# Chain sums of edge tiles by matrix products in a graph attention kernel's last loop bodies

## What is computed

```
q, k, v = layer_norm(x_node @ Wq), ... per head;  ke, ve = layer_norm(x_edge @ Wke), ...
rel_k = layer_norm(concat(ke, k[src]) @ relk_W + relk_b);  rel_v the same from ve, v
qk  = sum(q[dst] * rel_k, -1) / 4
m   = segment_max(qk, dst);  se = segment_sum(exp(qk - m[dst]), dst);  lse = log(se) + m
h   = (qk - lse[dst]) * rel_v
agg = segment_sum(h, dst)
z   = layer_norm(relu(agg @ z_W + z_b));   out = _layernorm(x + z)
```

## Time and profile before

| | us |
|---|---|
| median of 3 runs | 2994.78 (2994.47 to 2997.76) |
| profiled execution | 2993.24 |
| its span | 2991.5 |
| first instruction of `edges` (POOL) | 188.55 |
| first instruction of the tail (POOL's memset) | 2758.62 |
| first gather of sums | 2794.80 |
| first gather of log-sums | 2883.24 |

### The profile page before, as it was taken

The page is one execution under the profiler, slowest core; times in us unless marked ns, Lnnn a source line. Parts: engine busy times, 40 slices in busy tenths (PEclk is TensorE's granted clock), DMA queues, the critical chain, the costliest instruction groups (busy, mean ns, idle before and its releaser), DMA issues. The chain is left out here.

```text
span 2991.5 us, 74825 instructions
## 1 busy us (share of the span) xinstructions
PE 2805.4 (94%) x18870; PEld 2486.7 (83%) x18870; DVE 2848.9 (95%) x3072; ACT 2304.7 (77%) x5301; POOL 2396.4 (80%) x2622
## 2 busy tenths in 40 slices
PE   4669999999999999999999999999999999998945
PEld 3349999999999999999999999999999999996633
DVE  6879999999999999999999999999999999998948
ACT  2448888888888888888888888888888888886527
POOL 6768888888888888888888888888888888885773
PEclk8989999999999999999999999999999999999978
DMA  4568888888888888888888888888888888887742
GB/s 89 163 177 242 258 255 257 253 256 252 255 253 257 254 254 253 255 254 255 253 255 253 255 254 254 256 253 251 257 255 253 256 252 254 254 264 215 196 112 56
DMA packets 661200, 703.01 MB, mean 235 GB/s; under 512 B 98801, under 2 KB 555238, under 8 KB 660749
## 3 DMA queue, kind: packets, MB, share of 16 engines
q1 hardware_dynamic: 568897, 491.48, 54.4%
q0 software_dynamic: 84896, 208.11, 25.5%
q10 hardware_dynamic: 7340, 2.66, 0.5%
HBM read 470.00 MB, written 231.15 MB: 234 GB/s over the span
## 5 line engine op out<-in xcount | busy, mean ns | idle before, releaser
L1446 POOL DMA_INDIRECT e_rows<-node_table,e_gcol x1564 | 1911.9, 1222 | 420.2 <-issue 416.1
L1239 PE MATMUL banks<-w_edge,e_eat 128*128 128x240 f32 x6256 | 1397.0, 366 | 0.5 <-ACT e_ysq L1368 0.5
L1239 PEld LDWEIGHTS banks<-w_edge,e_eat 128*128 128x128 f32 x6256 | 1180.6, 190 | 84.5 <-issue 0.7
L1218 PE MATMUL banks<-e_h,e_oh 128*128 128x248 f32 x3128 | 782.9, 373 | 2.9 <-DVE e_h L1552 2.8
L1547 DVE TENSOR_REDUCE e_zs<-e_z 128x96 f32<-128x1440 f32 x391 | 642.7, 1644 | 0.2
L1218 PEld LDWEIGHTS banks<-e_h,e_oh 128*128 128x128 f32 x3128 | 563.5, 190 | 44.9 <-DVE e_h L1552 4.3
L1331 ACT ACTIVATE e_agg<-banks 128x496 f32<-128x496 f32 x782 | 458.0, 586 | 109.9 <-PE banks L1218 103.9
L1535 DVE TENSOR_TENSOR e_p<-banks,e_yr 128x960 f32<-128x960 f32 x391 | 452.5, 1157 | 27.6 <-PE banks L1239 13.7
L1552 DVE TENSOR_TENSOR e_h<-e_p,e_zw 128x960 f32<-128x960 f32 x391 | 449.5, 1150 | 1.2 <-POOL e_zw L1459 1.2
L1346 ACT ACTIVATE e_eat<-banks 128x512 f32<-128x512 f32 x391 | 233.4, 597 | 281.5 <-PE banks L1252 281.5
L1516 DVE TENSOR_TENSOR e_p<-e_p,e_rows 128x960 f32<-128x960 f32 x391 | 449.6, 1150 | 0.0
(11 more groups left out here) (414 smaller groups left out, 2607.2 us busy)
## 6 DMA issues: line engine op xcount, KB each, us to landing
tile_sums<-e_agg SPq DMA_DIRECT2D x391, 496.0 KB
e_q<-q_by_rank SPq DMA_DIRECT2D x1564, 90.0 KB
e_ea<-in_edge_attr SPq DMA_DIRECT2D x390, 256.0 KB
e_rows<-node_table,e_gcol POOLq DMA_INDIRECT x1564
edge_lse<-t_lse_sb SPq DMA_DIRECT2D x14, 448.0 KB, 3.5
edge_qk<-e_qkt SPq DMA_DIRECT2D x130, 48.0 KB
node_table<-n_tb SPq DMA_DIRECT2D x24, 240.0 KB, 2.6
n_x<-in_x SPq DMA_DIRECT2D x24, 128.0 KB, 2.3
```

Source lines behind the costliest of these rows:

```text
L1218: last = nc.tensor.matmul(sums_bank(x, loop, half)[:, (j % 2) * AW:(j % 2 + 1) * AW], oh[:, x % OR, j, :], hh[:, x % HR, j, :, :].rearrang ...
L1239: last = nc.tensor.matmul(out_ps[:, j // 2, (j % 2) * 2 * HC:(j % 2 + 1) * 2 * HC], eat[:, x % 4, j * P:(j + 1) * P], t["w_edge"][:, at:at ...
L1446: g.indirect_dma_start(out=rows[:, k, j, :], out_offset=None, in_=table, in_offset=bass.IndirectOffsetOnAxis(ap=gcol[:, kb, at:at + 1].bit ...
```

## The change

The scans over transposed rows give way to matrix products. Two matrices of 128x128 zeros and ones say for a set which of its tiles are in the same chain up to a tile, and which are in the chain that the last tile of the set before belongs to; they come by comparing a row of chain numbers (`seg_row`, the same in all partitions) with a column of them (`seg_col`, `last_col`). POOL makes them with 25 comparisons (`make_mats`), PE multiplies (`chain_sum`, one product for set 0 and two for the others), ACT copies the sums back over `firsts`, and POOL adds them to `tile_sums` (`add_set`). Sets 0 to 11 do this in bodies 391 to 400 and directly behind them, set 12 in the tail. The chain numbers are stored and loaded as a column in `start`; their broadcast to all partitions stands in body 385, and first rows are loaded two sets a body from there.

In the tail, the fourth load of scores waits for nothing, the fifth also for the last set's products (the matrices lie where it lands), the sixth for seven running maxima instead of the adds. The log-sum rows of the last three steps go to three pairs of banks: step 11 to banks 0 and 1, step 12 to 2 and 3, step 13 to 4 and 5. The last running sum stands ahead of the carries, the last two logarithms ahead of the last three copies.

```
 def chain_mats(t, k):
+    at = PARTS[3][1] * SUB + 2 * P * k
+    return t["x"][:, at:at + P], t["x"][:, at + P:at + 2 * P]
+def chain_sum(nc, t, k, bank):
+    same, last_same = chain_mats(t, k)
+    out = bank[:, (k % 2) * 2 * P:(k % 2) * 2 * P + AW]
+    done = nc.tensor.matmul(out, same, t["firsts"][:, k, :], start=True, stop=(k == 0))
+    if k:
+        done = nc.tensor.matmul(out, last_same, t["firsts"][:, k - 1, :], start=False, stop=True)
+def chain_copy(sc_, t, k, bank):
+    return sc_.activation(t["firsts"][:, k, :], bank[:, (k % 2) * 2 * P:(k % 2) * 2 * P + AW], mybir.ActivationFunctionType.Copy)
...
-CHAIN_AT = GROUPS + 3
+CHAIN_AT = GROUPS + 1
...
+                kk = 2 * (c - FIRSTS_AT)
+                if not loop and kk == 0:
+                    sp.dma_start(seg_row[:].rearrange("p k e -> p (k e)"), t["chain_d"].partition_broadcast(P)).then_inc(s_more, 16)
...
+            def chain_set(k):
+                pe.wait_ge(s_cl, k + 1)
...
+                if k:
+                    pe.wait_ge(s_cbc, k)
+                chain_sum(nc, t, k, agg_ps).then_inc(s_cs, 1)
...
-                if not loop and 0 <= c - CHAIN_AT < 4:
+                if not loop and c >= CHAIN_AT:
                     chain_set(c - CHAIN_AT)
...
+            def make_mats(k):
+                same, last_same = chain_mats(t, k)
...
+                ins = g.tensor_scalar(out=same, in0=seg_row[:, k, :], scalar1=seg_col[:, k:k + 1], scalar2=None, op0=ALU.is_equal)
+                if k:
+                    ins = g.tensor_scalar(out=last_same, in0=seg_row[:, k, :], scalar1=last_col[:, k - 1:k], scalar2=None, op0=ALU.is_equal)
+                ins.then_inc(s_cl, 1)
+            def add_set(k):
+                pool.wait_ge(s_cbc, k + 1)
+                pool.reg_add(last_sum, sums_less_2, 1)
+                chain_add(nc, t, k, last_sum).then_inc(s_add, 16)
...
+                k = c - GROUPS
+                if not loop and k >= 0:
+                    for k_ in range(2 * k, min(2 * k + 2, KT)):
+                        make_mats(k_)
+                    if k >= 2:
+                        add_set(k - 2)
             every(pool, body, GROUPS + 9)
+            for k in range(GROUPS + 9 - GROUPS - 2, KT - 1):
+                add_set(k)
...
-                if k == 3:
-                    sp.wait_ge(s_cb, 7)
                 if k == 4:
                     sp.wait_ge(s_m, 4)
+                    sp.wait_ge(s_cs, KT)
                 if k == 5:
-                    sp.wait_ge(s_add, 16 * KT)
+                    sp.wait_ge(s_m, 7)
...
+    def rows_bank(k):
+        return {NSUB - 3: 2 * ((NSUB - 2) % 2), NSUB - 2: 2 * ((NSUB - 1) % 2)}.get(k, 4)
...
             v.tensor_copy(out=ends[:, 0:1], in_=m[:, CE:CE + 1]).then_inc(s_end, 1)
+            run_sum(NSUB - 1)
+            dve.wait_ge(s_s, NSUB)
+            v.tensor_copy(out=ends[:, 2:3], in_=x[:, CE - 1:CE]).then_inc(s_end, 1)
...
-            run_sum(NSUB - 1)
-            dve.wait_ge(s_s, NSUB)
-            v.tensor_copy(out=ends[:, 2:3], in_=x[:, CE - 1:CE]).then_inc(s_end, 1)
...
+            ln_of(NSUB - 2)
+            ln_of(NSUB - 1)
+            copy_lse(NSUB - 3)
             act.wait_ge(s_ab, 2)
             sc_.activation(ab, ab, ACT.Exp).then_inc(s_abx, 1)
-            ln_of(NSUB - 2)
-            copy_lse(NSUB - 3)
-            ln_of(NSUB - 1)
             copy_lse(NSUB - 2)
```

More of the change, by code:

```diff
@@ L148, in chain_back @@
[L148 to L166, removed]
@@ L637, in _ @@
             v.tensor_copy(out=rank_o[:], in_=key_f[:, 0, :]).then_inc(s_ro, 1)
+            v.scalar_tensor_tensor(out=tq[:, 0, :], in0=key_f[:, 0, :], scalar=2.0, in1=linked, op0=ALU.mult, op1=ALU.add).then_inc(s_tq, 1)
             link(v.tensor_scalar(out=base[:], in0=loc[:, 1, :], scalar1=car_ps[:, 1:2], scalar2=None, op0=ALU.max))
@@ L1413, in body @@
                     nc.scalar.activation(zw[:, x % WR, :, :, 0], zln[:, :, 1:2 * H:2], ACT.Exp, scale=-0.5).then_inc(s_zw, 1)
-                if not loop and 0 <= c - CHAIN_AT < 4:
+                if not loop and c >= CHAIN_AT:
                     copy_set(c - CHAIN_AT)
             every(act, body, GROUPS + 10)
-            for kk in range(4, len(CHAIN_SETS)):
-                copy_set(kk)
-            for kk in range(4):
-                act.wait_ge(s_cb, kk + 1)
-                chain_copy(nc.scalar, t, (2 * kk, 2 * kk + 1), banks[:, 6 + kk % 2, :]).then_inc(s_cbc, 1)
+            for k in range(GROUPS + 10 - CHAIN_AT, KT - 1):
+                copy_set(k)
         @block.gpsimd
@@ L1501, in _ @@
             link(v.tensor_copy(out=p_f, in_=p_i[:, 1:3]))
+            link(v.scalar_tensor_tensor(out=last_col[:], in0=seg_col[:], scalar=1.0, in1=ident[:, P - 1:P].to_broadcast([P, KT]), op0=ALU.add, op1=ALU.mult))
+            link(v.tensor_scalar(out=last_col[:], in0=last_col[:], scalar1=-1.0, scalar2=None, op0=ALU.add))
             link(v.tensor_copy(out=same_c[:], in_=c_i))
@@ L1563, in _ @@
             every(dve, body, GROUPS + 9)
-            dve.wait_ge(s_more, 16)
-            dve.wait_ge(s_cc, 4)
-            for half in range(2):
-                chain_scan(v, t, 0, half).then_inc(s_cs, 1)
-            dve.wait_ge(s_cs, 2)
-            dve.wait_ge(s_cc, len(CHAIN_SETS))
-            for half in range(2):
-                chain_scan(v, t, 1, half).then_inc(s_cs, 1)
     ph.close([])
@@ L1690, in _ @@
             pool.reg_add(last_sum, sums_less_2, 1)
-            for k in range(KT):
-                pool.wait_ge(s_cbc, k // 2 + 1)
-                g.indirect_dma_start(out=t["sums_d"], out_offset=bass.IndirectOffsetOnAxis(ap=t["carry_idx"][:, k:k + 1].bitcast(u32), axis=0),
-                                     in_=back[:, k, :], in_offset=None,
-                                     bounds_check=last_sum, oob_is_err=True, compute_op=ALU.add).then_inc(s_add, 16)
+            pool.wait_ge(s_cbc, KT)
+            chain_add(nc, t, KT - 1, last_sum).then_inc(s_add, 16)
             pool.wait_ge(s_add, 16 * KT)
@@ L1799, in _ @@
                 v.tensor_tensor(out=ratio[:, k % RS, :], in0=ratio[:, k % RS, :], in1=fresh[:, lo:hi], op=ALU.add).then_inc(s_d, 1)
-                if k == 0:
-                    dve.wait_ge(s_cc, 7)
-                    dve.wait_ge(s_cs, 4)
-                    for half in range(2):
-                        chain_scan(v, t, 2, half).then_inc(s_cs, 1)
                 if k >= 1:
@@ L1981, in _ @@
             sc_ = nc.scalar
[L1982 to L1984 removed]
             load_fresh(3)
+            act.wait_ge(s_cs, KT)
+            chain_copy(sc_, t, KT - 1, bank[6]).then_inc(s_cbc, 1)
             act.wait_ge(s_bias, 1)
```

152 lines of the change are left out of this document (65 added, 87 removed).

## The result

The changed kernel takes 3008.94 us (median of 5 runs, 3007.68 to 3010.48), the kernel before 2994.78: 14.2 us more, a ratio of 1.0046 (95% interval 1.0035 to 1.0056). Forecast were 2987 and a range up to 2997. The time lies outside the range, and the sign is wrong too.

What follows compares the result with a forecast made beforehand. DVE and PE bound the loop; in the tail POOL decided when log-sum gathers begin. Gain 11.2 - 3 - 0.5 = 7.7 us gave 2985.5, with the runs' median 1.5 higher 2987; likeliest 2983 to 2990, 80% 2978 to 2997.

Steps and rivals of the forecast that it cites:

- Part 3: End of the edge loop: 28.6 us of new POOL work against 25.8 free, so the tail starts 3 us later.
- Part 2: Log-sums in the tail: their last store decides, first log-sum gather 113.3 us after the tail's start instead of 124.5.
- T0: Start of the tail, DVE's first memset there; 2758.7 us before, forecast 3 us later.
- (a): POOL's new work overruns the loop's end: tail starts 14 to 18 us later, time 2998 to 3002; chance 0.12.
- (d): POOL's comparisons and DVE's instructions exclude each other at the loop's end: 7 us more, time 2994; chance 0.20.
- the gap: DVE near the tail's eighth step, ended by PE: a loss of 5.3 us from the third score load's new wait.
- the end's gain: End of the tail: three pairs of banks let the last log-sum copy end 3.5 us earlier.
- the room of 0.3: Slack in us between the third log-sum copy's end and PE's start on the next rows, subtracted from the delay.
- the start of the tail: Chain scans leave DVE, two products join PE: taken as zero, bounds 2 us of gain and 1 of loss.
- Part 1: POOL's tail: twelve of 13 adds leave, gathers of sums run from 12 to 108 us after the tail's start.
- G: First log-sum gather in the tail, forecast 113.3 us after the tail's start, with 108.3 from there to the end.
- Part 4: The rest: a store, a load and three tiny DVE instructions early on cost 0.5 us.

Runs made afterwards that it cites:

- experiment 3: The changed kernel without the sixth load's wait for the seventh running maximum; 3001.87 us, ratio 1.0023 to the kernel before.
- mended versions: Five variants of the changed kernel without the sixth load's new wait, last set's product behind the first step, comparisons and adds placed differently; 2988.16 to 2992.72 us.
- experiment 4: The changed kernel with the last set's product and its copy behind the tail's first log-sum step, run twice; 2998.59 and 3000.46 us.

## Why the forecast was wrong

**Part 3 is the step that failed most**, by 9.8 of some 22 us, and Part 2 second, by 8.0. With Part 3 right and the rest as measured the time would still have been about 2999, past the range. Part 3 failed by price and by window. The price: "I take 0.40" for a comparison, with 0.67 as the upper bound. Alone it takes 0.60; in the queue 0.89, as in five of the seven bodies one or two stand behind `e_h` or the row addition. 25 cost 22.3 us and not 10. The adds were priced well (1.3 in a body, forecast 1.55). The window: I set 28.6 us of work against 25.8 free in the stretch up to T0, but 15.9 of these lie behind POOL's last small product, where comparisons, which PE needs before, and half of the adds can't use them. Before that product there was this (window; its length, POOL's busy us and count; clock, DMA):

```profile
2712.70:2742.70 30.00, 17.90 (x24) 1.00 0.57 181
```

12.1 us were free. Ahead of it came 22.3 us of comparisons and six adds of 1.3 to 2.0, 8.5: 30.8 in all, 18.7 more than was free. DVE's last `e_h` was 18.2 us later. (The match is closer than the count deserves: 9.5 of the 12.1 are waits for ACT, the rest are gaps at issues, which a comparison can't fill, while small products that had been stretched to 1.1 to 2.0 us no longer were.)

With my own two prices in the right window the sum would have been 10 + 9.3 - 12.1, so 7.2 us late instead of the 2.8 that I had: the window is 4.4 us of the miss. The price of the comparison is 12.3, of which 5.0 are the 0.60 and 7.3 the meetings with DVE; the adds give back 0.8.

T0 moved by 12.6 only (without the 3.4 from before the loop), since 10.3 us and not 15.9 lie between that `e_h` and T0. I had allowed at most 1 us for this. SP's last issue came 7.6 us behind the last `e_h` instead of 14.2; ACT's wait of 3.87 us for a store and DVE's last two chain scans, in front of which it had waited 4.01 us for ACT, are gone. Which of the two gives how much isn't shown.

**Rivals (a) and (d)** were one mechanism. Rival (d) had the lock-step right and its size too: 7 us, measured 7.3. The way to it was another: it counted a chance of 0.46 a comparison and 0.6 us each, while the meeting occurs in every body here in which POOL has no wait left and its comparisons stand right behind the product that releases `e_h`, and costs nearly the whole of `e_h`, 1.2 us of it. That agrees with the rule of the Trainium skill, "SBUF — State Buffer", section "Who interferes with whom", that a DVE instruction with two SBUF inputs and a GpSimd instruction that reads SBUF exclude each other. The rival's T0, 10 us late, and its 2994 fell short because the 0.40, the window and the tail stayed as forecast in its sum. Rival (a) had the size of T0 and the right verdict on it (14 to 18, measured 15.9 with 3.4 from before the loop), but I gave it 0.12 and put its condition at the wrong place: what counts is the room up to POOL's last small product, not the sum up to T0. That its T0 came true is partly luck, since its adds of 2.25 us took 1.3; and its time, 2998 to 3002, stayed 7 us short, as it had none of the tail's losses.

**Part 2.** Right: the log-sums' last store decides, the gap's place, the wait of 8 us, the end's gain (3.9; forecast 3.5), and by experiment 3 that the sixth load's wait causes the gap. Mis-sized: the gap, 9.1 and not 5.3. The store was released 6.0 us later in the stage (forecast 5.6) and took 8.1 (forecast 7.7), less the room of 0.3 makes 6.1. The missing 3 are PE's clock, by the windows above: after the wait that the change makes, the next rows took 6.0 us instead of the 3.2 that I carried over from a busy PE. Experiment 3 removes wait and aftermath together, so this split rests on the windows alone. I had priced the wait and not what stands behind it at the lower clock. Missed: the start of the tail, 5.0 us of loss against a bound of 1. I took the load's landing for a store's 3.5 us; it took 7.9, and I had put PE's wait in front of everything in the change's order without pricing it.

**Part 1.** The gathers of sums began at T0 + 20.4 and ended at T0 + 114.7, not 12 and 108. This cost nothing in the changed kernel, but it is what bounds all mended versions (G = T0 + 112.4 to 114.2).

**Part 4.** +3.4 in the profile, forecast 0.5; about 2 by the mean of all profiles, and its cause stays open. The stretch from G to the end, which I carried over as 108.3, was 109.9; over all fourteen profiles it lies between 108.3 and 114.0, and what moves it isn't shown.

## What to carry to other kernels

Free time of an engine counts only ahead of the last thing that others wait for; measure it to that instruction, not to the end of the stage. Work put on an idle engine right behind a small product that releases another engine's long instruction meets this instruction in every body in which the idle engine has no wait left, so it is priced with it, and put on the engine that does it fastest: here 25 comparisons cost DVE, the busiest engine, 7.5 us and POOL 22. A wait of PE is priced with the products behind it at the lower clock. A load that was just issued should not be waited for at the head of a queue; but one step of other work hides it only if it lands in time, which it did in one of two executions here and in the other missed by 5.76 us.

## What was not expected of the hardware

A comparison of 128x128 fp32 with a scalar per partition takes 0.60 us on POOL and 0.28 to 0.32 on DVE, while a select of the same shape on POOL takes 0.31. An indirect add shows a span of 1.6 us, but POOL's next instruction starts 1.11 to 1.16 after the add's start, and small products behind it show spans of 0.8 instead of 0.25 while they start 0.24 apart: the durations shown there overlap and can't be summed. PE came out of an idle time of 6.32 us at the lower clock (0.51 in the next 6.0 us) and was back at 1.00 after it, so that a wait cost half as much again as its length. And one load of 27 KB, issued close behind larger ones, let PE go on 7.9 us after its issue in the changed kernel and 14.6 in the first profile of experiment 4; adds landed after up to 10.4.
